# The maximum of an attention unit's scores, taken in two halves and joined

## What is computed

```python
C_q = Q @ Wq_d                                  # Q = x: 4 x 512 x 1024 -> 128
C_kv = K @ Wkv_d                                # K = context: 4 x 1601 x 1024 -> 64
CqWqk = (C_q @ W_qk).reshape(b, n, 16, 64)
scores = jnp.einsum('bnhl,bkl->bhnk', CqWqk, C_kv) / 8
attn = jax.nn.softmax(scores, axis=-1)          # over 1601 keys
V_up = (C_kv @ Wv_u).reshape(b, nkv, 16, 64)
out = jnp.einsum('bhnk,bkhd->bnhd', attn, V_up)
```

## Time and profile before

| | |
|---|---|
| median of three runs | 2830.6 us |
| the profiled execution: span | 2825.3 us |
| the median over that span | 5.3 us |
| TensorE busy in the span (matmul ends modelled) | 94% |
| VectorE | 80% |
| GpSimd | 69% |
| ScalarE | 59% |
| mean granted TensorE clock | 0.977 of full speed |
| first and last maximum (L1129) start at | 368.0 and 1492.5 us |

### The profile page before, as it was taken

How to read it: one execution, slowest core, us unless ns; L and a number is a source line. 1 busy time by engine, 2 the same in 40 slices (tenths; PEclk the granted TensorE clock), 3 DMA queues, 4 the chain that set the end, 5 groups by cost and what they waited for, 6 DMA issues and landing times. The chain is left out here.

```text
span 2825.3 us, 41267 instructions
## 1 busy us (share of the span) xinstructions
PE 2646.3 (94%) x14360; PEld 1994.5 (71%) x14360; DVE 2262.4 (80%) x2150; ACT 1680.2 (59%) x2635; POOL 1940.3 (69%) x1423
## 2 busy tenths in 40 slices
PE   6988989999999999999997999999999999999997
PEld 3655656666666666666665788888888888788885
DVE  1644668888887788778875899999999899899988
ACT  2343567777777777777775554445445555555553
POOL 1000457767777777767774888888887788888883
PEclk9888989999999999999998999999999999999999
DMA  7224766766677677677764222221222222232221
GB/s 257 94 91 154 229 221 204 231 193 203 205 230 219 210 213 219 209 234 232 227 203 141 105 90 93 86 75 68 69 78 96 95 88 84 67 120 75 75 97 75
DMA packets 166768, 420.60 MB, mean 149 GB/s; under 512 B 30113, under 2 KB 57634, under 8 KB 166050
## 3 DMA queue, kind: packets, MB, share of 16 engines
q1 hardware_dynamic: 164258, 409.57, 46.4%
q10 hardware_dynamic: 2304, 8.39, 0.7%
HBM read 248.43 MB, written 75.04 MB: 114 GB/s over the span
## 5 line engine op out<-in xcount | busy, mean ns | idle before, releaser
L1656 DVE SCALAR_TENSOR_TENSOR c_acc<-c_ps,c_sd,c_acc 128x1024 f32<-128x1024 f32 x448 | 573.1, 1282 | 95.2 <-PE c_ps L1503 95.1
L1233 POOL COPY b_pt<-b_tn 32x640 f32<-32x640 f32 x640 | 457.0, 714 | 268.6 <-DVE b_tn L1135 236.9
L1561 ACT ACTIVATE c_scaled<-c_ps,c_sgu 128x1024 f32<-128x1024 f32 x336 | 375.3, 1117 | 420.8 <-PE c_ps L1503 418.8
L1129 DVE TENSOR_REDUCE b_nm<-b_sc 128x1 f32<-128x1604 f32 x256 | 468.1, 1828 | 190.5 <-PE b_sc L964 189.3
L1046 ACT ACTIVATE b_pr<-b_sc,b_nm 128x799 f32<-128x799 f32 (+1 forms) x512 | 476.5, 933 | 240.3 <-DVE b_nm L1129 215.8
L1743 POOL TENSOR_TENSOR c_sum_u<-c_sum_u,c_scaled 128x1024 f32<-128x1024 f32 x168 | 404.7, 2409 | 107.9 <-ACT c_scaled L1561 107.5
L1743 POOL TENSOR_TENSOR c_sum_g<-c_sum_g,c_scaled 128x1024 f32<-128x1024 f32 x168 | 405.1, 2411 | 81.9 <-ACT c_scaled L1561 81.7
L964 PE MATMUL b_sc<-b_kh,b_qs 128*128 128x402 f32 (+1 forms) x1024 | 404.4, 395 | 41.1 <-ACT b_pr L1046 37.4
L983 PE MATMUL b_po<-b_pt,shared 128*64 128x256 f32 x2560 | 392.3, 395 | 32.5 <-DMA b_pt<-b_tn 32.4
L1135 DVE STREAM_TRANSPOSE b_tn<-b_pr 128x1280 f32<-128x1280 f32 x256 | 384.8, 1503 | 6.8 <-DMA b_pt<-b_tn 2.9
L964 PE MATMUL b_sc<-b_kl,b_qs 128*128 128x402 f32 (+1 forms) x1024 | 358.6, 350 | 0.0
(11 more groups left out here) (194 smaller groups left out, 4387.3 us busy)
## 6 DMA issues: line engine op xcount, KB each, us to landing
b_pt<-b_tn SPq DMA_DIRECT2D x1152, 80.0 KB, 2.6
c_uw_int<-wint_u SPq DMA_DIRECT2D x56, 512.0 KB, 3.5
c_gw_int<-wint_g SPq DMA_DIRECT2D x56, 512.0 KB, 3.4
c_dw_int<-wint_d SPq DMA_DIRECT2D x56, 512.0 KB, 3.4
a_cx<-in_b_ctxT SPq DMA_DIRECT2D x16, 1608.0 KB, 10.1
b_rw<-in_c_gw SPq DMA_DIRECT2D x28, 512.0 KB, 4.2
b_rz<-in_c_gz SPq DMA_DIRECT2D x28, 512.0 KB, 5.5
b_rw<-in_c_uw SPq DMA_DIRECT2D x28, 512.0 KB, 4.0
```

The costliest lines, as they stand in the source:

```text
L1129: V.tensor_reduce(nm[:, u % 2:u % 2 + 1], both, AXY, ALU.max, negate=True).then_inc(s_nm, 1)
L1233: G.tensor_copy(pt[s][32 * c:32 * c + 32, a, :, :], tn[s][32 * a:32 * a + 32, c, :, :]).then_inc(s_block, 1)
L1561: S.activation(dst[:, :], pair[SLOT[x, t] % 4][:, :], ACT.Identity, scale=scale(x, t)).then_inc(s_e, 1)
L1656: V.scalar_tensor_tensor(out=total, in0=pair[SLOT[x, t] % 4][:, :], scalar=scale(x, t), in1=total, op0=ALU.mult, op1=ALU.add).then_inc(s_a ...
```

## The change

The reduction over both halves is split. A new `first_maximum(u)` reduces the first half's 802 columns into its own column of `b_nm_first`. It is called for unit 0 ahead of the loop and for unit `k + 1` behind `turn(k - 1)`, ahead of `norm_piece(k)`. `maximum(u)` now reduces the second half alone (799 columns) into `b_nm_second`, waits on a new semaphore for both reductions, which VectorE itself raises, and takes the smaller of the two negated columns into `b_nm`. The wait for the exponentials of unit `u - 2` stands ahead of that minimum. In `mixer` the two semaphores of the small activations become one, on which VectorE waits for 1 and then for 2.

```diff
-            S.activation(alog[:, :], alog[:, :], ACT.Exp).then_inc(s_aexp, 1)
-            S.activation(g1[:, :], g1[:, :], ACT.Sigmoid).then_inc(s_gexp, 1)
+            S.activation(alog[:, :], alog[:, :], ACT.Exp).then_inc(s_gates, 1)
+            S.activation(g1[:, :], g1[:, :], ACT.Sigmoid).then_inc(s_gates, 1)
...
-            V.wait_ge(s_aexp, 1)
+            V.wait_ge(s_gates, 1)
             V.tensor_scalar(alog[:, :], alog[:, :], -1.0, None, ALU.mult)
-            V.wait_ge(s_gexp, 1)
+            V.wait_ge(s_gates, 2)
...
+        nm0 = sb("b_nm_first", [P, 2])
+        nm1 = sb("b_nm_second", [P, 2])
...
+            def first_maximum(u):
+                at = half_at(u, 0)
+                V.wait_ge(s_sc, 2 * u + 1)
+                V.tensor_reduce(nm0[:, u % 2:u % 2 + 1], sc[:, at + SIDE[0][0]:at + SIDE[0][1]], AX, ALU.max,
+                                negate=True).then_inc(s_part, 1)
+
             def maximum(u):
-                first, second = half_at(u, 0) + SIDE[0][0], half_at(u, 1) + SIDE[1][0] - 3
+                at, j = half_at(u, 1), slice(u % 2, u % 2 + 1)
                 V.wait_ge(s_sc, 2 * u + 2)
+                V.tensor_reduce(nm1[:, j], sc[:, at + SIDE[1][0]:at + SIDE[1][1]], AX, ALU.max, negate=True).then_inc(s_part, 1)
+                V.wait_ge(s_part, 2 * u + 2)
                 if u >= 2:
                     V.wait_ge(s_ex, 2 * u - 2)
-                both = bass.AP(sc, min(first, second), [[3 * 1024, P], [abs(second - first), 2], [1, 802]])
-                V.tensor_reduce(nm[:, u % 2:u % 2 + 1], both, AXY, ALU.max, negate=True).then_inc(s_nm, 1)
+                V.tensor_tensor(nm[:, j], nm0[:, j], nm1[:, j], ALU.min).then_inc(s_nm, 1)
...
+            first_maximum(0)
             for k in range(NU + OUT_AT):
                 if k < NU:
                     maximum(k)
...
                 if 1 <= k <= NU:
                     turn(k - 1)
+                if k + 1 < NU:
+                    first_maximum(k + 1)
                 if k < NU:
                     norm_piece(k)
```

More of the change, by code:

```diff
@@ L80, in mixer @@
         s_down, s_gelu, s_xmid = sem("down"), sem("gelu"), sem("xmid")
-        s_clamp, s_aexp, s_gexp, s_ones, s_half, s_prep = (sem(n) for n in ("clamp", "aexp", "gexp", "ones", "half", "prep"))
+        s_clamp, s_gates, s_ones, s_half, s_prep = (sem(n) for n in ("clamp", "gates", "ones", "half", "prep"))
         s_z, s_sz, s_dt = sem("z"), sem("sz"), sem("dt")
@@ L790, in attention @@
         s_sc, s_nm, s_ex, s_tt = (sem(n) for n in ("scores", "nm", "ex", "turned"))
+        s_part = sem("nm_part")
         s_move, s_block, s_cross = [sem("move0"), sem("move1")], sem("block"), sem("cross")
```

## The result

| | before | changed |
|---|---|---|
| median | 2830.6 us | 2844.61 us (2841.72 to 2847.03, five runs) |
| ratio, 95% interval | | 1.0055 (1.004 to 1.007) |
| the profiled execution: span | 2825.3 us | 2839.9 us |
| first to last (second) maximum | 1124.5 us | 1136.0 us |

A forecast was written before the change was run, and what follows sets the result against it. A loop through TensorE, VectorE and ScalarE was taken to bound the attention stage. Busy pairs +20, free pairs -11, statistics +8, DMA stalls -2 and merged semaphores 0 gave about +14 us: 2845 us, range 2806 to 2866.

The forecast's parts named there:

- The loop: TensorE scores, VectorE maximum, ScalarE exponential set the attention stage's pace: 4.06 us per ordinary unit, 3.45 after the split.
- E from M: Start of second-half maximum on VectorE to start of first exponential on ScalarE: 1.33 us forecast instead of 1.94, before any hold.
- w: Time the joining minimum on VectorE waits for what GpSimd has left of its running instruction; mean 0.47 us in busy eights.
- The hold: VectorE's minimum of two SBUF columns stands until GpSimd's running instruction ends, delaying the exponential and the transpose behind it.
- The walk: Step-by-step timing of eight attention units: 34.8 us with GpSimd's subtraction in each pair, 32.8 with copies alone, 32.4 unheld.
- The sum: All terms for the whole kernel added: +14 us, median 2830.6 becoming 2845.
- the moves by DMA: Stalls where the weighing waits for block moves, 44.8 us in 42 waits before; forecast to change by -2 us.
- busy and free eights: Eight-unit stretches with GpSimd's subtraction and cast (21, +20 us in total) or with copies alone (11, -11 us).
- statistics: 24 VectorE pieces of 0.65 us, coming to stand between first and second maximum: a third of a microsecond each, +8 us.
- the forecast's 0.60: Chance given to the main case, a held minimum with small waits, spread 2833 to 2857 us.
- the last case: Slower by more: VectorE's own wait costs 0.30 us or GpSimd's copies slip; +30 to +35, 2863 us, chance 0.12.
- The rival "not held": GpSimd doesn't block the minimum: walk -45, statistics +8, DMA moves late oftener +10; -27, 2804 us, chance 0.20.

The follow-up runs named there:

- e4_before_pointer: Kernel before, its whole maximum followed by a join of the column with itself, one tensor input and a scalar column: 2864.51 us, 1.0114.
- e1: Changed kernel with the two columns joined by a one-tensor-input operation, the first half's column as per-partition scalar: 2810.38 us, 0.9925 of the kernel before.
- e2: Changed kernel with both halves' columns side by side, joined by a reduction over two elements: 2808.11 us, 0.9913 of the kernel before; repeats 2811.7 and 2811.88.
- e3: Kernel before, its whole maximum followed by a minimum of the column with itself as two tensor inputs: 2904.99 us, 1.0257.
- e7: Split kernel with the join as two-element reduction, but the first half's reduction waits for both halves' scores: 2884.24 us, 1.0187 of the kernel before.
- e8: Changed kernel with GpSimd's subtraction and cast each run as two halves of 512 columns: 2837.27 us, 1.0012 of the kernel before.
- e9: Changed kernel with GpSimd's subtraction of the low key parts run as six pieces of up to 268 columns: 2832.92 us, 1.0003 of the kernel before.

## Why the prediction was right, point by point

**The loop.** Right. E from M is 0.98 + 0.03 + w + 0.16 + 0.11; only the wait on VectorE's own semaphore was 34 ns where 70 were taken. e4_before_pointer shows the loop responding one for one (4.06 to 4.30). The first part of the forecast, a shorter loop, is shown by e1 and e2.

**The hold.** Right in kind and mean. The prediction took w = 0.27 in odd units; measured over the busy pairs 0.30. In even units it had 0.47, 1.13, 0.47, 0.58 for the units 0, 2, 4 and 6 (mean 0.66); measured 0.50, 1.10, 0.48, 0.63 (mean 0.68). In free pairs the even units, taken at 0, stood 0.16, nearly all of it two of the three long ones.

**The walk.** The second maxima of the changed kernel from unit 16 on (timeline of VectorE):

```profile
438.03 0.98 DVE L1135 TENSOR_REDUCE b_nm_second<-b_sc 128x1 f32<-128x799 f32 x1
...
442.03 0.98 DVE L1135 TENSOR_REDUCE b_nm_second<-b_sc 128x1 f32<-128x799 f32 x1
...
446.02 0.98 DVE L1135 TENSOR_REDUCE b_nm_second<-b_sc 128x1 f32<-128x799 f32 x1
...
451.23 0.97 DVE L1135 TENSOR_REDUCE b_nm_second<-b_sc 128x1 f32<-128x799 f32 x1
...
455.26 0.98 DVE L1135 TENSOR_REDUCE b_nm_second<-b_sc 128x1 f32<-128x799 f32 x1
...
458.83 0.99 DVE L1135 TENSOR_REDUCE b_nm_second<-b_sc 128x1 f32<-128x799 f32 x1
...
464.32 0.98 DVE L1135 TENSOR_REDUCE b_nm_second<-b_sc 128x1 f32<-128x799 f32 x1
...
469.06 0.97 DVE L1135 TENSOR_REDUCE b_nm_second<-b_sc 128x1 f32<-128x799 f32 x1
...
472.82 0.99 DVE L1135 TENSOR_REDUCE b_nm_second<-b_sc 128x1 f32<-128x799 f32 x1
```

The steps are 4.00, 3.99, 5.21, 4.03, 3.57, 5.49, 4.74, 3.76, in all 34.8. The walk had 3.95, 3.95, 5.21, 3.75, 3.91, 5.64, 4.66, 3.75, in all 34.8, with the 5.21 in unit 2 where the rows of before have 4.28. The steps agree within 0.35 us each; that the sums do is helped by luck, since one pair of this eight is free (at the 3.57) and the walk has four busy ones. For the unheld join it had 32.4. Of e2_reduce_join's eights, counted from unit 0, the shortest behind the first runs from 843.51 to 876.14, 32.6; the median eight is 34.0, so the walk gives the best case:

```profile
843.51 0.98 DVE L1134 TENSOR_REDUCE b_nm_halves<-b_sc 128x1 f32<-128x799 f32 x1
...
876.14 0.98 DVE L1134 TENSOR_REDUCE b_nm_halves<-b_sc 128x1 f32<-128x799 f32 x1
```

**The sum.** Its total hit within 1 us, and that is partly luck: two of its terms were wrong in opposite ways. Left out: GpSimd's key split, a subtraction of 3.58 us, which holds three minima, +10.6 us between the maxima. It stood in the code as `split_keys` and in the trace of before, and the prediction counted only the instructions that repeat. Mis-sized: the moves by DMA, put at -2 us; TensorE's weight loads wait 33.6 us for them instead of 44.8, -11. Taking 11.5 as the stage's measured difference, the rest (busy and free eights, statistics, together +17 in the sum) comes to 11.5 - 10.6 + 11.2 = 12. So these terms were some 5 us high together. The timelines separate them in part. Against before, the three eights with the key split are 9.8 us longer, the six with three or four statistics pieces 7.5 (the sum had +8 for the pieces, but busy and free pairs lie in these eights too), the other twenty-two together 7.6 shorter, moves by DMA included, and the steps behind them 1.8 longer. The walk's gain and loss of busy and free eights can't be told from the DMA's in this. And all of it rests on one execution of each kernel: the kernel of e2_reduce_join was profiled three times and took 1099.4, 1111.4 and 1107.3 us from first to last maximum, so a term of 5 us is within what executions differ by.

**The chances** have a slip: half of the forecast's 0.60 with the last case's 0.12 is 0.42 for slower, where 0.46 stands.

**The rival "not held"** was a true picture of another kernel: 2804 was its price, 2808 to 2812 were measured when the join had one tensor input. Its DMA term was too small: +29 us of waits instead of +10. The waits of TensorE's weight loads for the moves grow with the pace: 7.4 us at 2905 (e3), 24.3 at 2884 (e7), 23.6 at 2865 (e4), 33.6 at 2845, 43.1 at 2837 (e8), 33.1 at 2833 (e9), 44.8 at 2831, 69.6 at 2810 (e1), 73.9 at 2808 (e2). Of these e9, 33.1 at 2833, falls clearly out of the order. A faster loop gets back only part of what it gains.

## What to carry to other kernels

In this kernel an instruction of VectorE with two tensor inputs in SBUF took its own time only where GpSimd was idle: begun under a running GpSimd instruction it ended with that. On a path that sets the pace, give it a form with one tensor input (a scalar column, or a reduction over neighbouring columns), and look for GpSimd's rare long instructions as well as for its many short ones. When a value is taken ahead, ask when its input is ready: here the lead was one instruction long, and that was worth 73 us.

## What the runs showed of the hardware

- A 128x1 minimum of two SBUF columns took 0.16 us free and up to 3.56 us under a GpSimd instruction; its end followed GpSimd's by 6 to 25 ns in 181 cases, with GpSimd's copies on 32 partitions as with its 128-partition operations. After a block copy the minimum got through before the next copy of the five, which starts 0.06 us behind the end of the last; it never stood under two.
- Six minima that began within 4 ns of a copy's start took 0.16 us, and their copies 753 to 762 ns instead of 715.
- VectorE's subtractions of the queries' low parts (`b_qs<-b_mi,b_qs`), with one tensor input in PSUM and one in SBUF, took 683 to 694 ns in all 64 cases of the changed kernel, 55 of them begun under a GpSimd instruction. Two tensor inputs alone don't make the hold.
- The same join as an operation with a scalar column took 0.214 us and as a reduction over two elements 0.155 us, all 256 times within 6 ns.
- Where VectorE waited on its own semaphore, the next instruction started 33 to 36 ns behind the end of the last.
- A reduction of 802 columns of PSUM took 0.946 to 0.995 us, and a next instruction that waited for nothing started 0.88 to 0.91 after its start.
